# A one-core gated cross-attention and expert block: loads reordered behind the first transposes, and the other rows' queries made a step later

## The reference, cut to what matters

```python
x = x + tanh(g_xattn[0]) * xattn(layernorm(x), ctx_1024, Wq, bq, Wk, bk, Wv, bv, Wo, bo)
x = x + tanh(g_ffn[0]) * ffn(layernorm(x), router_w, expert_bias, w_gate, w_down, ...)

def xattn(x, context, ...):          # 16 heads of depth 8
    q = x @ Wq.T + bq; k = context @ Wk.T + bk; v = context @ Wv.T + bv
    attn = softmax(q k^T / sqrt(8)); return (attn v) @ Wo.T + bo

def ffn(x, ...):                     # 160 experts, the 8 best of each token, all computed
    combine = top-8 weights of sigmoid(x @ router_w.T + expert_bias), times 2.5, else 0
    routed = sum_e combine[:, e] * silu(x @ w_gate[e].T) @ w_down[e].T
    return routed + silu(x @ w_gate_shared.T) @ w_down_shared.T
```

## Time and profile before

| | |
|---|---|
| median of 3 runs | 1125.85 us |
| the profiled execution, time | 1124.83 us |
| its span, first to last instruction | 1123.2 us |
| mean granted TensorE clock | 0.990 |
| busy: PE, DVE, ACT, POOL | 95%, 86%, 75%, 53% |
| shares of the chain that ended last | PE 75%, DVE 12%, issue 4%, queue SP 3% |

### The profile page before, as it was taken

One profiled execution on the slowest core, in us unless ns is written; L12 is line 12 of the kernel. 1 busy time (PEld: TensorE's weight loads), 2 busy tenths in 40 slices (PEclk: granted clock), 3 DMA queues, 4 the chain that ended last, 5 costly groups with the idle time before them and its releaser, 6 DMA issues.

```text
span 1123.2 us, 37415 instructions
## 1 busy us (share of the span) xinstructions
PE 1068.0 (95%) x12142; PEld 708.1 (63%) x12142; DVE 963.5 (86%) x1699; ACT 847.6 (75%) x1817; POOL 591.7 (53%) x984
## 2 busy tenths in 40 slices
PE   2799999999999999999999999998999999999998
PEld 1366777777777777777777777654455555555554
DVE  4678888888888888888888888578999999999998
ACT  3476777777777777777777776687888888888887
POOL 5798887887888888788888886320000000000000
PEclk9799999999999999999999999999999999999999
DMA  8778777577577576676676652482788778777873
GB/s 159 158 166 214 145 178 179 123 184 170 133 186 170 131 186 162 142 185 152 152 185 142 150 132 67 110 207 97 229 228 226 226 236 237 229 229 227 230 237 118
DMA packets 229501, 197.12 MB, mean 175 GB/s; under 512 B 161039, under 2 KB 207263, under 8 KB 229462
## 3 DMA queue, kind: packets, MB, share of 16 engines
q1 hardware_dynamic: 218036, 173.22, 61.8%
q0 software_dynamic: 9200, 21.85, 6.9%
q10 hardware_dynamic: 2226, 1.56, 0.7%
HBM read 109.96 MB, written 12.55 MB: 109 GB/s over the span
## 4 chain that ended last, share of the span: by engine, by line
PE 75%; DVE 12%; issue 4%; SPq 3%; ACT 2%; DMA 2%; DVEq 0%; POOL 0%; ACTq 0%
PE bank L1550 15%; PE bank L1540 15%; PE bank L1343 12%; PE bank L1377 11%; PE bank L1358 10%; DVE part_max L1030 6%; PE bank L1413 5%; PE bank L1401 4%; DVE rec L1169 2%; PE bank L1457 1%; SPq L369 1%; DMA ctx_in<-in_ctx_dram 1%; SPq L405 1%; DVE o_raw L1044 1%; DVE kparts L1160 1%
## 5 line engine op out<-in xcount | busy, mean ns | idle before, releaser
L800 ACT ACTIVATE p_exp<-bank 125x448 f32<-125x448 f32 x768 | 400.1, 544 | 183.9 <-PE bank L1358 182.9
L1030 DVE TENSOR_REDUCE part_max<-bank 128x1 f32<-128x500 f32 x672 | 420.1, 671 | 62.0 <-PE bank L1377 61.5
L1358 PE MATMUL bank<-q_st,k_stk 97*125 97x224 f16 x1536 | 272.6, 261 | 2.5 <-ACT p_exp L800 1.9
L1377 PE MATMUL bank<-kparts,q_blk 128*128 128x500 f16 x672 | 255.8, 384 | 17.5 <-DVE part_max L1030 13.2
L1358 PEld LDWEIGHTS bank<-q_st,k_stk 97*125 97x125 f16 x1536 | 195.9, 138 | 66.2 <-ACT p_exp L800 13.1
L867 ACT ACTIVATE ctT<-bank 128x448 f32<-128x448 f32 x320 | 174.2, 545 | 40.9 <-DVE v_sb L1203 9.8
L1210 DVE TENSOR_TENSOR ctT<-v_sb,ctT 128x448 f16<-128x448 f32 (+1 forms) x324 | 200.4, 619 | 0.2
L1550 PE MATMUL bank<-ctT,w_ring 128*128 128x448 f16 x816 | 198.9, 352 | 0.1
L874 ACT ACTIVATE ctT<-v_sb 128x448 f16<-128x448 f32 x320 | 182.2, 569 | 7.0 <-DVE v_sb L1203 6.9
L1343 PE MATMUL bank<-p_exp,v_sb 125*25 125x168 f32 (+1 forms) x6144 | 186.2, 262 | 0.4 <-ACT p_exp L800 0.4
L1343 PEld LDWEIGHTS bank<-p_exp,v_sb 125*25 125x25 f32 x6144 | 142.1, 103 | 42.6 <-ACT p_exp L800 0.5
(11 more groups left out here) (193 smaller groups left out, 1376.3 us busy)
## 6 DMA issues: line engine op xcount, KB each, us to landing
k_stk<-kparts SPq DMA_DIRECT2D x384, 93.8 KB, 4.1
v_sb<-c_scratch SPq DMA_DIRECT2D x68, 448.0 KB, 4.3
k_stk<-c_scratch SPq DMA_DIRECT2D x68, 448.0 KB, 4.3
ctx_in<-in_ctx_dram SPq DMA_DIRECT2D x30, 672.0 KB
w_scratch<-w_out POOLq DMA_DIRECT2D x80, 128.0 KB, 3.2
w_in<-in_L_ffn_w_gate_dram POOLq DMA_DIRECT2D x80, 64.0 KB, 3.7
w_in<-in_L_ffn_w_down_dram POOLq DMA_DIRECT2D x80, 64.0 KB, 4.1
v_sb<-c_scratch SPq DMA_DIRECT2D x8, 336.0 KB, 3.8
```

Source lines behind the costliest of these rows:

```text
L800: act.activation(p_exp[0:KP, j % PR, f * 448:(f + 1) * 448], ST[f][0:KP, 0:448], ACT.Exp).then_inc(exp_done, 1)
L1030: v.reduce_max(part_max[:, i // NCH, i % NCH:i % NCH + 1], SM[i % NSM][:, 0:CK], axis=AX.X).then_inc(sm_maxed, 1)
L1358: last = pe.matmul(ST[f][0:KP, (g % 2) * GC:(g % 2 + 1) * GC], k_stk[0:97, u, g, j * KP:(j + 1) * KP], q_st[0:97, u, g, :, :].rearrange("p ...
L1377: pe.matmul(SM[i % NSM][:, 0:CK], rows, kparts[:, u, 0, c * CK:(c + 1) * CK], start=True, stop=True).then_inc(sm_done, 1)
```

## The change

It puts all three chunk loads of batch 0 ahead on queue SP and the four weights on ScalarE's queue. The loads of batch 1 and of the other rows leave ScalarE's queue and go onto SP, behind the three first transposes. GpSimd's early constants come before its first splits. The rest is centred in three parts in step 1 (slots 5, 7, 9) and squared in slot 10, scaled at (2, 1), and its three chunks are transposed at (2, 3), (2, 7), (2, 11) and multiplied at (2, 4), (2, 8), (3, 0), now in `KB`. For that TensorE waits for `k_lo_done` before each transposing and, before the next keys, for `q_lo_done`. The stacking is spread over the ends of SP's steps 3, 4 and 5; GpSimd waits for it before step 6; six steps are written out.

```diff
-    VAR_REST_AT, RSTD_REST_AT, SCALE_REST_AT = (1, 1), (1, 2), (1, 3)
-    TOKENS_REST_AT = {(1, 5): (1, 3), (1, 8): (3, 4)}
-    Q_REST_AT = {(1, 6): (1, 3), (1, 9): (3, 4)}
...
+    CENTRE_REST_AT, SQUARE_REST_AT = {(1, 5): 1, (1, 7): 2, (1, 9): 3}, (1, 10)
+    VAR_REST_AT, RSTD_REST_AT, SCALE_REST_AT = (1, 11), (2, 0), (2, 1)
+    TOKENS_REST_AT = {(2, 3): (1, 2), (2, 7): (2, 3), (2, 11): (3, 4)}
+    Q_REST_AT = {(2, 4): (1, 2), (2, 8): (2, 3), (3, 0): (3, 4)}
+    Q_HI_REST_AT = {(2, 4): (1, 2), (2, 8): (2, 3), (3, 0): (3, 4)}
+    Q_LO_REST_AT = {(2, 5): (1, 2), (2, 9): (2, 3), (3, 1): (3, 4)}
+    KEYS_BEHIND = {(2, 6): 2, (2, 10): 3, (3, 2): 4}
...
-        REST_ROWS_AT = {2: (0, 2, 1)}
-        QB = [bank[0], bank[0], bank[1], bank[0]]
+        REST_ROWS_AT = {3: (0,), 4: (2,), 5: (1,)}
+        QB = [bank[0], KB, KB, KB]
...
-            for s in range(first, 4):
+            for s in range(first, 6):
...
-            with eng.Fori(2, loop_to // 2) as h:
+            with eng.Fori(3, loop_to // 2) as h:
...
         @block.sync
...
-            load_chunk(0)
-            for n, w in enumerate((Wq, Wk, Wv, Wo)):
-                sp.dma_start(w_raw[:, n, :], w).then_inc(weights_in, 16)
-            for c in range(1, NCH):
+            for c in range(NCH):
                 load_chunk(c)
...
             for c in range(NCH):
                 transpose_ctx(0, c, c + 1, None)
+            load_rows(sp, ctx_here[1], ctx_in[0:KP, 1, :, :], ctx[1].rearrange("(p j) c -> p j c", j=KT))
+            stack_queries(0, 1, (0,), q_rows)
+            load_x(sp, *REST, x_rest)
+            stack_queries(0, 1, (1,), q_rows)
+            transpose_chunks((0, 0), (0,))
             load_ctx((0, 0))
-            stack_queries(0, 1, (0, 1), q_rows)
-            transpose_chunks((0, 0), (0,))
             stack_queries(0, 1, (2,), q_rows)
...
         @block.gpsimd
...
-            attention(pool, body, B - 2, {2: first_pairs, 3: add_constant, 4: all_rows})
+            attention(pool, body, B - 2, {2: first_pairs, 3: add_constant, 6: all_rows})
...
         @block.scalar
...
+            for n, w in enumerate((Wq, Wk, Wv, Wo)):
+                act.dma_start(w_raw[:, n, :], w).then_inc(weights_in, 16)
...
-            load_x(act, *REST, x_rest)
-            load_rows(act, ctx_here[1], ctx_in[0:KP, 1, :, :], ctx[1].rearrange("(p j) c -> p j c", j=KT))
...
-            square_rest()
...
         @block.vector
...
-            dve.wait_ge(x_rest, 32)
-            centre(*REST)
...
+            def centre_rest(c):
+                dve.wait_ge(x_rest, 32)
+                centre(c * PPC, (c + 1) * PPC)
...
         @block.tensor
...
                     if c:
-                        pe.wait_ge(q_lo_done, 2 if c == 3 else 1)
+                        pe.wait_ge(k_lo_done, 2 * NCH + c)
                     transpose_tokens(c, QB[c])
...
                         until(pe, k_lo_done, b * NCH + c)
+                        if isinstance(step[0], int) and (b, k) in KEYS_BEHIND:
+                            pe.wait_ge(q_lo_done, KEYS_BEHIND[(b, k)])
```

More of the change, by code:

```diff
@@ L69, in flamingo_gated_block @@
     FIRST, REST = (0, PPC), (PPC, NP)
-    VAR_REST_AT, RSTD_REST_AT, SCALE_REST_AT = (1, 1), (1, 2), (1, 3)
-    TOKENS_REST_AT = {(1, 5): (1, 3), (1, 8): (3, 4)}
-    Q_REST_AT = {(1, 6): (1, 3), (1, 9): (3, 4)}
-    Q_HI_REST_AT = {(1, 7): (1, 3), (1, 10): (3, 4)}
-    Q_LO_REST_AT = {(1, 8): (1, 3), (1, 11): (3, 4)}
+    CENTRE_REST_AT, SQUARE_REST_AT = {(1, 5): 1, (1, 7): 2, (1, 9): 3}, (1, 10)
[5 more added lines that the diff above has]
+    KEYS_BEHIND = {(2, 6): 2, (2, 10): 3, (3, 2): 4}
     SHARED_AT, GATES_AT, CONSTANT_AT, QUERIES_FREE_AT, OUT_FREE_AT = (2, 0), (2, 1), (2, 2), (2, 1), (2, 4)
@@ L276, in attention @@
                 body((s // 2, s % 2))
-            if 4 in before:
-                before[4]()
-            with eng.Fori(2, loop_to // 2) as h:
+            if 6 in before:
+                before[6]()
+            with eng.Fori(3, loop_to // 2) as h:
                 body((h, 0))
@@ L600, in add_constant @@
                 pool.wait_ge(constant_made, 1)
-                pool.wait_ge(ln_sub, 2)
+                pool.wait_ge(ln_sub, NTC)
                 pool.tensor_tensor(xt[:, :, :], xt[:, :, :], bo_b[:, :].unsqueeze(1).to_broadcast([PT, NP, D]),
                                    ALU.add).then_inc(pre_done, 1)
-            pool.wait_ge(pad_here, 32)
-            for c in range(NCH):
-                split_ctx((0, 0), c)
             const(pool.memset(den_spread[:, :], 0.0))
@@ L615, in _ @@
             assert made[0] == K_ONES
+            pool.wait_ge(pad_here, 32)
+            for c in range(NCH):
+                split_ctx((0, 0), c)
             const(pool.memset(v_sb[:, :, :, 0:4, 3 * d:VW], 1.0))
@@ L736, in square_rest @@
             def square_rest():
-                act.wait_ge(ln_sub, 2)
+                act.wait_ge(ln_sub, NTC)
                 for p in range(*REST):
@@ L805, in body @@
                             values(back(step, 1), k // TPC)
-                    aside(step, k, (VAR_REST_AT, lambda: root(2, *REST)), (SCALE_REST_AT, scale_rest),
+                    aside(step, k, (SQUARE_REST_AT, square_rest), (VAR_REST_AT, lambda: root(2, *REST)), (SCALE_REST_AT, scale_rest),
                           *((at, lambda c=c: query_tokens(*c)) for at, c in TOKENS_REST_AT.items()),
@@ L1052, in body @@
                                         negate=True).then_inc(neg_made, 1)
-                    aside(step, k, (VAR_REST_AT, variance_rest), (RSTD_REST_AT, rstd_rest),
+                    aside(step, k, *((at, lambda c=c: centre_rest(c)) for at, c in CENTRE_REST_AT.items()),
+                          (VAR_REST_AT, variance_rest), (RSTD_REST_AT, rstd_rest),
                           *((at, lambda c=c: queries(*c)) for at, c in Q_LO_REST_AT.items()),
@@ L1319, in queries_free @@
             def queries_free():
-                pe.wait_ge(q_hi_done, NTC)
-                pe.wait_ge(q_lo_done, NTC)
+                pe.wait_ge(q_hi_done, 1)
+                pe.wait_ge(q_lo_done, 1)
                 pe.wait_ge(k_ones, 32)
```

## The result

The changed kernel takes 1142.05 us (median of 4 runs, 1137.70 to 1143.17) against 1125.26 us of the kernel before (4 runs, 1122.21 to 1126.08). The ratio is 1.0147, 95% interval 1.0114 to 1.0181: 16.8 us slower by the two medians. The forecast was slower, 1138.0, with a range of 1129 to 1145. The profiled execution of the changed kernel is its fastest, 1137.7 us with a span of 1136.2; before it was 1124.83 with 1123.2. So the two traces explain 13.0 us of the difference. The other 3.8 us lie between executions (see e12). One execution further down, the third of e1, took 2155.03 us and is left out of every number.

What follows compares the result with a forecast made beforehand. TensorE's own work was taken to set the pace of the attention steps. Terms -3.0 + 11.2 + 1.4 - 1.5 + 4.0 = +12.1 on 1124.83 gave 1136.9 profiled, median 1138.0 us, range 1129 to 1145.

Steps and rivals of the forecast that it cites:

- step 2 starts: Start and step 1: reordered loads bring batch 1's keys at 27.0 and step 2 at 50.4, 3.0 us gained.
- steps 2 and 3, with the clock: Moved query work and TensorE's waits there cost 11.2 us, bounds 3.8 and 13; lowered granted clock adds 1.4.
- stackings: Spreading the twelve stackings from the end of SP's step 2 gains 1.5 us, bounds 0 to 1.5.
- GpSimd's wait: Before step 6 GpSimd waits for the last stacking, delaying step 7's scores: 4.0 us lost, bounds 0 and 5.
- rival 4: Repeated waits keep the clock at 1.2 GHz through step 2, 6 to 7 us more: 1144; chance 0.12.
- Rival 5: At the start, loads fail to help and batch 1's keys stay at 32.7: 5.7 us more, 1143.7; chance 0.06.
- squares, then four `wo_m` DMAs, only then the last keys: End of step 1: ScalarE's squares (3.5 us), four DMA issues (2.6), then keys (0.7) put step 2 23.4 after batch 1's keys.
- Rival 2: In steps 2 and 3 work costs 3.8 us but waits nothing: 1125.1, no change; chance 0.06.
- rival 1: Slack in steps 2 to 7 hides the waits and moved work, GpSimd catches up: 1121.3, faster; chance 0.09.
- Writing out two steps: Writing out two more steps costs 0, since straight and looped steps go at one pace.
- rival 3: GpSimd runs far enough ahead, so its wait and the clock cost nothing: 1132.6; chance 0.14.
- the median stands 1.0 above it: Whole kernel: the runs' median lies 1.0 us above the profiled execution, forecast 1136.9, giving 1138.0.

Runs made afterwards that it cites:

- e12: The changed kernel run once more, unaltered, for a second profile: 1142.43 us, ratio 1.0161 to the kernel before.
- e1: The changed kernel with the last part of the other rows' stacking at the end of SP's step 4 instead of 5: 1134.9 us, ratio 1.0095.
- e11: The kernel of e1 with twelve of sixteen `wo_m` DMAs moved to slots 0 and 1 of step 1: 1134.74 us, ratio 1.0097.
- e5: The kernel of e1 with the other rows loaded just ahead of batch 1 and centred, squared, scaled early in step 1: 1133.97 us, ratio 1.0087.
- e8: The kernel before with weights on ScalarE's queue, chunks together on SP's, and the centring behind the first low keys: 1124.66 us, ratio 1.0007.
- e3: The kernel before with only the stackings spread over SP's steps 3 to 5, six steps written out, GpSimd waiting before step 6: 1128.91 us, ratio 1.0045.
- e4: The kernel before with only six steps written out in place of four: 1123.9 us, ratio 0.9995.
- e6: The kernel of e5 with the other rows' tokens and queries in step 1 too, in banks 0 and 1: 1123.53 us, ratio 0.9994.
- e7: The kernel of e1 with products nobody reads put where TensorE waits, around the start of step 2: 1134.27 us, ratio 1.0090.
- e2: The changed kernel's loads with the other rows' tokens and queries left in step 1, stackings in step 2 as before: 1129.33 us, ratio 1.0049.

## Why the prediction was right

The sum, term by term, each as the prediction put it, with what the trace of the changed kernel shows.

| term | forecast | measured | from |
|---|---|---|---|
| step 2 starts | -3.0 (50.4) | -5.6 | 53.47, 47.90 |
| steps 2 and 3, with the clock | +11.2 +1.4 | +14.1 | start of step 2 to batch 2's row: 42.16 before, 56.24 after |
| stackings | -1.5 | -1.5 | batches 2 to 6: 84.78 before, less two pairs of 41.63 |
| GpSimd's wait | +4.0 | +6.1 | batches 4 to 6: 47.77, less 41.63 |
| sum | +12.1 | +13.1 | spans: +13.0 |

The mechanisms hold, but that the sum came within 1.0 is partly luck: the start came out 2.6 better than forecast, steps 2 and 3 1.5 worse and GpSimd's wait 2.1 worse. The measured median, 4.0 above the forecast one, lies nearer to the numbers of rivals 4 and 5 (1144 and 1143.7), whose mechanisms the traces rule out.

*Start.* First keys at 11.94 (12.6 forecast), batch 1's at 25.74 (27.0). From there to step 2 it took 22.2 (23.4 forecast). The last centring was done 16.7 after the keys, as worked out (16.6). The step that was mis-sized is "squares, then four `wo_m` DMAs, only then the last keys": ScalarE's queue issued the DMAs while its last squares still ran (from 44.42, the squares to 46.0), so they delay the evacuation by 1.1 and not 2.6; e11, without them, shows no delay. The chain of waits names GpSimd's `q_blk` (done at 47.45) ahead of step 2's first product, but the product waits for the last keys' evacuation too, and that ended last (47.81, the product at 47.90). It is the same in e1, e5, e11 and the kernel before: the product starts 0.1 after the evacuation. That the gain comes from the bytes put behind, as the sum had it, e8 shows. Its size is less certain. The same code starts step 2 at 47.90, 48.25 (e12) or 50.14 (e1), and the kernel before's at 53.47, 50.88 (e3) or 51.39 (e4). Against e3 and e4 the term would be 3.0 to 3.5, as forecast, and the next one 15.4 to 15.8 in place of 14.1, since from the start of step 2 to batch 2's row they take 40.9 and 40.4.

*Steps 2 and 3.* The waits were foreseen one by one: 4, 1.4 and 0.9 ahead of the transposes against 5.28, 1.51 and 0.94, and three times 0.6 ahead of the next keys against 0.51, 0.73 and 0.51. The work takes 4.0 by the starts of what follows each piece (0.77 + 0.41 + 0.41 for the transposes, three times 0.81 for the products), forecast 3.8. Together, less the 0.8 waited before: 12.7, so 1.4 of the 14.1 is left over. It has the size of the clock's term, but isn't shown to be it. Row to row, step 2 took 33.9 us where it was 21.7, and step 3 21.4 where it was 20.6. That the scaling is the head of the 5.28 is read from the chain of waits, and e5 supports it (the constant term 2.5 sooner after the step's start); its price alone wasn't measured. e6 against e5 shows the whole bill of the queries in step 2, 10.4. Rival 2 (work costs, waits don't) and rival 1 (all hidden) fall by these rows and runs.

*Clock.* Granted 0.84 and 0.83 in 50 to 70, not 0.5 through the step as rival 4 had it. e7 bought the clock back and 1.1 us between two rows, nothing measurable in all. But the clock had been low in the kernel before as well, 0.85 over its step 2 against 0.87 now, so +1.4 as a loss against it isn't borne out; e7's 1.1 is what a full clock gave back there.

*GpSimd.* The prediction had the mechanism and its place, but gave 4.0 and a bound of 5; it was 6.1 in the trace (7.0 in e12's and 7.5 in e3's, by the same rows) and 5.9 to 7.2 by e1's ratio and median. Its own terms add up to a last issue at 142.9 and not 142.5, which would have made 4.4. Of its steps, GpSimd's 21.5 from the stacking to the end of `q_st` were right (153.72 to 175.14 is 21.4), and TensorE's idle time of 4.3 too. The step that fell short: the idle time of one engine was taken for the whole price. What follows such a stop was left out: the granted clock was 0.77 in 174 to 178, and ScalarE and VectorE, too, had nothing to do meanwhile. How the other 1.8 us divide between these wasn't tried. GpSimd's idle time before it was 15.25, not 9: it had run further ahead and waited for the maxima until 142.67 anyway, and the stacking's part is the 11 us from there. e3 shows the mechanism alone, in a kernel without the late steps 2 and 3, so rival 3 falls.

*The median.* The profiled execution came within 0.8 of the forecast for it (1137.7, 1136.9). The step "the median stands 1.0 above it", taken from the kernel before, didn't carry over: here it stands 4.3 above. The range held it.

*Rival 5* (the loads don't do what they should) falls by 25.74. Had the change been only the first two edits of the loads it would have held, as e8 shows. Writing out two steps: 0, by e4.

## What to carry to other kernels

Work that sits in a stretch where the bounding engine waits costs little; moved into a stretch where it doesn't, it costs itself and, if it borrows a buffer that the main stream uses, a wait on every exchange (here 9.5 us of waits at six exchanges for 4 of work; the longest, 5.3, hangs on the moved scaling too). Compare two traces of one code before reading a difference between two kernels: here they differ by 2 to 4 us in the first steps. Before a wait is moved behind a queue's later work, look at what that queue waits for: a stacking at the end of step 5 was really a stacking after step 6's row of maxima, and it cost 6 us. A load that is put back to free the bandwidth takes its whole chain of consumers with it, and in e2 what was won at the first keys was lost there.
